# Moving one reciprocal ahead of nine calls on VectorE, and one normalisation ahead of one subtraction on GpSimd

## The reference, cut to what matters

```
x = x + layernorm(attention(layernorm(x)))        # softmax attention, 16 heads of width 16
x = x + layernorm(ffn(layernorm(x)))              # 256 -> 1024, gelu, 1024 -> 256, ternary weights
x = x + layernorm(gated_linear_attention(layernorm(x)))
x = x + layernorm(experts(layernorm(x)))          # 8 experts, the best 2 of each token, and a shared one
```

## Time and profile before

| | |
|---|---|
| time, median of 3 runs | 2177.56 us (2175.62 to 2183.19) |
| time of the profiled execution | 2177.89 us |
| its span, first to last instruction | 2176.1 us |
| granted clock of TensorE, mean over the span | 0.966 |
| TensorE busy over the span | 94% |
| VectorE, ScalarE, GpSimd busy | 69%, 59%, 29% |
| attention (from the first to the last unit's division) | up to about 813 us |
| feed-forward stage, TensorE's first to last matmul | 787 to 955 us |

### The profile page before, as it was taken

How to read it: one execution, slowest core, us unless ns; L and a number is a source line. 1 busy time by engine, 2 the same in 40 slices (tenths; PEclk the granted TensorE clock), 3 DMA queues, 4 the chain that set the end, 5 groups by cost and what they waited for, 6 DMA issues and landing times. The chain is left out here.

```text
span 2176.1 us, 41968 instructions
## 1 busy us (share of the span) xinstructions
PE 2043.0 (94%) x16610; PEld 1458.8 (67%) x16610; DVE 1505.4 (69%) x2451; ACT 1283.8 (59%) x2555; POOL 625.1 (29%) x481
## 2 busy tenths in 40 slices
PE   7999999999999979956999999999999999769997
PEld 6643333333333348955888888888888888658997
DVE  7889999999999867953546464646464644466775
ACT  3258888888888856744444444444444444346664
POOL 1200000000000034524334342425251615224544
PEclk9889999999999999977999999999999999979999
DMA  6732322222322222133112121212121212032321
GB/s 230 237 53 60 76 66 60 77 69 57 82 66 64 71 65 79 48 113 126 59 60 78 60 79 60 78 61 80 57 82 48 91 36 93 11 116 108 117 108 69
DMA packets 95545, 176.72 MB, mean 81 GB/s; under 512 B 19736, under 2 KB 57648, under 8 KB 90224
## 3 DMA queue, kind: packets, MB, share of 16 engines
q1 hardware_dynamic: 95344, 173.98, 26.1%
HBM read 134.49 MB, written 38.67 MB: 80 GB/s over the span
## 5 line engine op out<-in xcount | busy, mean ns | idle before, releaser
L731 DVE TENSOR_REDUCE att_sb_mx<-att_ps_psM 128x1 f32<-128x1024 f32 x512 | 624.1, 1221 | 27.9 <-PE att_ps_psM L944 25.1
L1149 ACT ACTIVATE att_sb_pt<-att_ps_psSO 128x512 f32<-128x512 f32 x1024 | 557.1, 597 | 95.1 <-PE att_ps_psSO L962 40.5
L944 PE MATMUL att_ps_psM<-stack_sb_k,stack_sb_q 48*128 48x512 f32 x1024 | 381.5, 454 | 5.5 <-DVE att_sb_mx L731 4.0
L962 PE MATMUL att_ps_psSO<-stack_sb_q,stack_sb_k 50*128 50x512 f32 x1024 | 373.5, 444 | 0.5 <-DMA stack_sb_q<-att_sb_mrow 0.5
L974 PE MATMUL att_ps_psSO<-att_sb_pt,stack_sb_v 128*32 128x256 f32 x4096 | 326.4, 391 | 8.6 <-ACT att_sb_osb L1142 8.6
L962 PEld LDWEIGHTS att_ps_psSO<-stack_sb_q,stack_sb_k 50*128 50x128 f32 x1024 | 153.1, 185 | 202.4 <-ACT att_sb_pt L1149 155.5
L2171 ACT ACTIVATE gla_sb_sg<-gla_ps_psP 128x512 f32<-128x512 f32 x64 | 38.3, 599 | 312.5 <-PE gla_ps_psP L1933 312.5
L974 PEld LDWEIGHTS att_ps_psSO<-att_sb_pt,stack_sb_v 128*32 128x32 f32 x4096 | 82.0, 108 | 192.1 <-issue 102.9
L2505 POOL TENSOR_TENSOR gla_sb_dm<-gla_sb_dm,gla_sb_masked 128x1024 f32<-128x1024 f32 x64 | 159.4, 2512 | 97.4 <-DMA gla_sb_dm<-decay_rows 97.4
L944 PEld LDWEIGHTS att_ps_psM<-stack_sb_k,stack_sb_q 48*128 48x128 f32 x1024 | 156.8, 189 | 19.3 <-DVE att_sb_mx L731 16.3
L2188 ACT ACTIVATE gla_sb_dm<-gla_sb_dm,gla_sb_neg_g 128x128 f32<-128x128 f32 x512 | 156.3, 391 | 6.3 <-POOL gla_sb_dm L2505 6.3
(11 more groups left out here) (261 smaller groups left out, 4704.8 us busy)
## 6 DMA issues: line engine op xcount, KB each, us to landing
gla_sb_dm<-decay_rows SPq DMA_DIRECT2D x32, 1024.0 KB, 6.3
qk_parts<-stack_sb_part SPq DMA_DIRECT2D x32, 512.0 KB, 3.3
gla_sb_eg<-decay_exp SPq DMA_DIRECT2D x64, 256.0 KB, 6.6
moe_sb_gb<-gate_rows SPq DMA_DIRECT2D x8, 2048.0 KB, 7.3
stack_sb_q<-qk_parts SPq DMA_DIRECT2D x192, 64.0 KB, 2.9
stack_sb_k<-qk_parts SPq DMA_DIRECT2D x96, 128.0 KB, 4.3
att_sb_rb<-sums SPq DMA_DIRECT2D x32, 256.0 KB
attended<-att_sb_on SPq DMA_DIRECT2D x32, 256.0 KB, 4.8
```

Of the source, the lines that this page charges most:

```text
L731: nc.vector.tensor_reduce(mx[:, qh, 8 * r + c:8 * r + c + 1], psM[:, t % 2, :], AX.X, ALU.max).then_inc(maxima_taken, 1)
L944: mm = pe.matmul(psM[:, t % 2, c * ST:(c + 1) * ST], q[rs, g, qh, j, n * P:(n + 1) * P], k[rs, g, j, c * ST:(c + 1) * ST], start=True, sto ...
L962: pe.matmul(psS[:, ring_slot(pos), :], k[rs, g, j, s * P:(s + 1) * P], q[rs, g, qh, j, :], start=True, stop=True).then_inc(ring_done, 1)
L1149: nc.scalar.activation(pt[:, s % (LAG + 2), ORDER[i], :], psS[:, (pos + 1) % 3, :], ACT.Exp, scale=AD ** -0.5).then_inc(ring_taken, 1)
```

## The change

Two calls are moved; no instruction is added or removed.

```diff
             split_hidden(0, 0)
+            reciprocal(2 * NBG - 1, 1)
             normalize_x1(1)
             split_hidden(0, 2)
             below(1, f_.w2)
...
             take_projected(2)
             stats_of_projected(2)
             split_hidden(0, 6)
-            reciprocal(2 * NBG - 1, 1)
             add_projected(2)
...
                 split_hidden(i, 3)
-                split_hidden(i, 5)
                 if i == 0:
                     normalize(BATCH - 1, NG - 1, 1)
+                split_hidden(i, 5)
                 if i + 2 < NST:
                     norm_of_projected(i + 2)
```

## The result

The changed kernel took 2169.32 us in the median of 5 runs (2167.17 to 2174.38), the kernel before beside it 2177.84 us (2175.62 to 2183.19). The ratio is 0.9947, with a 95% interval of 0.9928 to 0.9966. The forecast was 2170.0 us (2166.5 to 2173.0), a gain of 7.6 us. The two medians are 8.5 us apart (a ratio of 0.9961, inside the interval), and the one after sits 0.7 us from the forecast. The ratio's middle puts the gain at 11.5 us (7.4 to 15.7 of 2177.56), more than was forecast, and the time at 2166.0 us, just under the range.

A forecast was written before the change was run, and what follows sets the result against it. Feed-forward stage bound by TensorE, except a hole of 11.94 us bound by a wait. Statistics at 805.5 plus 2.0 us put ScalarE's shift at 807.5 instead of 815.05: 7.6 us off, no clock gain, 2170.0 us (2166.5 to 2173.0).

The forecast's parts named there:

- The chain: Feed-forward stage: TensorE waits for gelu, ScalarE's shift, POOL's power, last unit's normalisation, its transfers and VectorE's late reciprocal; 11.94 us.
- The move on POOL: Split of block 5 put behind the last unit's normalisation: worth nothing by itself, slips 0.4 us, at worst 1.8 us.
- When the reciprocal runs: On VectorE after the first split: last unit's reciprocal at 792.4 us, waiting 0.6 us for `den`; bounds 791.77 and 793.0.
- The slip on VectorE: Statistics of supertile 2 come 0.75 us later, at 805.5 us, through the wait and POOL collisions; bounds 0 and 2.1 us.
- From the statistics to the shift: From supertile 2's statistics through POOL's power to ScalarE's shift: 2.0 us, so the shift starts at 807.5, not 815.05.
- the hole: TensorE's stop in the feed-forward stage, between 806 and 818 us: to shrink from 11.94 to some 4.3 us.
- The clock: TensorE's clock after its stop: still falls to 0.50, no gain counted, bounds 0 and 3 us.
- the sum: ScalarE's shift at 807.5 in place of 815.05 us: 7.6 us off the end, bounds 6.2 and 8.7 us.
- The row that the term went by: Profile row of a 4.35 us TensorE stop ending at 1935.61: clock at 0.50 before TensorE had resumed.
- The range: Whole kernel: 2166.5 to 2173.0 us, from the clock rival's 2167 less median scatter up to the collisions' 2172.7.

The follow-up runs named there:

- reciprocal alone: Changed kernel with the move on POOL taken back, so only the reciprocal is moved against the kernel before: 2171.8 against 2180.49 us, ratio 0.9957.
- exchanged order: Changed kernel with the 512 KB load of the residual input issued behind the small transfer of the sums: 2171.97 against 2180.28 us, ratio 0.9963.
- filled holes: Dummy matmuls where TensorE stops, 48 in the kernel before (2177.79 against 2180.49 us), 15 in the changed kernel (2172.51 against 2180.28 us).
- the first four experiments: Changed kernel repeated, reciprocal moved alone, normalisation moved alone, power ahead of normalisation with the reciprocal late: ratios 0.9950, 0.9957, 1.0004, 0.9962 against the kernel before.
- changed again: The changed kernel once more with no edit, beside the kernel before: 2171.58 against 2180.49 us, ratio 0.9950.
- power first: Kernel before, reciprocal left late, the last unit's normalisation put behind the power and split of block 7 on POOL: 2171.89 against 2180.28 us.

## Where the prediction held, and which terms were off

**The chain.** Confirmed in each link: the stage is 164.8 us with the reciprocal left late and the power ahead of the normalisation, the whole gain. With the normalisation moved alone it is 176.8 us, no gain, with the reciprocal alone 164.9 us. The move on POOL was put at nothing, with a cover of 1 us; the run without it has POOL idle for 1.07 us.

**When the reciprocal runs.** Told as 792.4, measured 793.03, at the upper bound of 793.0. The forecast took over the issue at 788.38 from the kernel before, and in the changed kernel SP issued the transfer at 788.91, 0.5 us later. From issue to start it took 4.1 us, under the 4.5 us of the unit before. SP's issue of the load ahead took 1.19 us in this execution; why, stays open. The last packets on the wires, from which 792.4 was worked out, can also be those of the load: with the exchanged order the reciprocal ran at 791.74 with the traffic still going on.

**The slip on VectorE.** Told as 0.75 us (0 to 2.1), measured 0.2 to 0.3 us. The term was summed as if every collision with POOL had to be paid. Measured, part of POOL's first split passed during the wait of 1.04 us: the L148 took 1.65 us in place of 2.35 us, the ternary step 2.35 us in place of 3.25 us, and only L760 grew, from 1.27 to 2.29 us. The idle time took the place of collisions.

**From the statistics to the shift.** Told as 2.0 us; 807.07 - 805.06 = 2.0 us. The power beside the split took 1.39 us as told. The shift came 8.0 us sooner and the hole became 8.1 us shorter, for 7.6 us forecast.

**The clock.** This is the term of the sum that was mis-sized, and the step that failed in it: from "the clock falls again" it followed "no gain", as if a fall cost the same after a short stop as after a long one. The clock fell, but was low for 3.5 us of work in place of 6 us: the projection came 9.1 us sooner where the shift came 8.0 us sooner. The other 1.1 us are the clock. By the filled holes the term is 3.1 - 1.6 = 1.5 us, within its own bounds of 0 and 3 us; with the 7.7 us of the rest it makes the 9.2 us. The row that the term went by showed a fall inside a stop of 4.35 us; in the stop of 3.82 us the clock held to the end and fell as TensorE resumed. The second profile of the kernel before shows that this isn't the change's own: there the same long hole was followed by the shorter low stretch. Against that profile the stage gains 7.6 us, against the first 9.2 us; the mean is 8.4 us.

**The range.** It gave the median's own scatter 1 us. The 26 runs of the kernel before beside the first four experiments went from 2176.8 to 2187.2 us; an estimate by drawing five of them again and again is that one median of 5 scatters by 1.9 us (one standard deviation), and a difference of two by 2.7 us. The interval of the first ratio is 0.38% wide, 8 us. The step "a microsecond for the median's own scatter" is what put the ratio's middle outside the range: of its 11.5 us, 7.6 us were forecast, 1.6 us more are in the stage (the clock above all), and the other 2.3 us are seen in no profile of the stage. The differences of medians in the three runs of the changed kernel or its near equals (changed again, reciprocal alone, power first) are 8.9, 8.7 and 8.4 us, against 8.4 us in the stage; so the 11.5 us of the first ratio can be the 8.4 us and scatter, and no second mechanism is needed. This is argued from the sizes, not shown. That the first median lies within 0.7 us of the forecast is in part luck, since a difference of two such medians scatters by 2.7 us. That the falls of the clock in the next stage make a good part of this scatter is shown in size (2.1 us each, 0 to 5 in a profile), and so are the two places where they come; what decides whether one comes, and whether their number depends on the change, stays open. If the difference in the means were real, the change would give back over 2 us, and the medians of the whole don't show it.

## What to carry to other kernels

An operation that nobody needs soon can still set the end if it waits at the head of an in-order list: ask for each wait what stands behind it, and compare the time at which that was ready. The cure can be either to make the awaited thing early or to put it behind the urgent one, and the second needed no change on another engine. When two engines hold each other up, a wait can be almost free and its removal almost worthless (1.04 us of wait were worth 0.2 us); only the time at which the next engine is released counts. And a gain of 1 us in a kernel whose runs scatter by 10 us is measured in the length of its stage, not in the median of the whole, with each kernel profiled twice: two profiles of the same kernel differed by 1.6 us in this stage.

## What the runs showed of the hardware that was not expected

TensorE's granted clock fell to half for between 3 and 4 us, 0 to 5 times in the same stage of 940 us, at a cost of about 2.1 us each. 30 of 37 falls came in the middle of dense work, all of them where 128x16 matmuls give way to 128x512 ones, and 7 behind one stop of about 2 us. After the same stop of nearly 12 us it was low for 6 us of work in one execution and for some 2.9 us in another of the same kernel. Filling the stops with dummy matmuls kept it at 1.00 there, worth 3.1 us (1.5 us against the second profile) and 1.6 us of the stage. A transfer of 8 KB issued behind a load of 512 KB came late mostly because SP was still issuing the load, 1.0 us, and less on the wires, where at least 0.3 us are shown.
